# A graph network layer pair on one core: two neighbour runs per couple of units, a longer gather ring at the start, and a late stage cut into pieces

## What is computed

```python
hsrc = h[src]; coef = w_comp[etype]                    # 8 bases, 32 relations
msg = sum_b (hsrc @ weight[b]) * coef[:, b]            # times norm, one number per edge
node = relu(segment_sum(msg * norm, dst) + bias)
x = layernorm(x + node)
neigh = segment_sum(x[src] + edge_attr, dst)
h = ((1 + eps) * x + neigh) @ W1 + b1                  # 256 columns
h = relu(batchnorm(h) * gamma + beta)
out = layernorm(x + h @ W2 + b2)
```

## Time and profile before

| | |
|---|---|
| median of 3 runs | 603.48 us (603.25 to 607.04) |
| profiled execution, its time | 605.07 us |
| profiled execution, span | 603.3 us |
| PE busy | 507.7 us, 84% |
| DVE busy | 458.3 us, 76% |
| POOL busy | 401.1 us, 66% |
| ACT busy | 218.0 us, 36% |
| granted PE clock, mean | 0.885 |

### The profile page before, as it was taken

The page is one execution under the profiler, slowest core; times in us unless marked ns, Lnnn a source line. Parts: engine busy times, 40 slices in busy tenths (PEclk is TensorE's granted clock), DMA queues, the critical chain, the costliest instruction groups (busy, mean ns, idle before and its releaser), DMA issues.

```text
span 603.3 us, 12767 instructions
## 1 busy us (share of the span) xinstructions
PE 507.7 (84%) x3965; PEld 429.8 (71%) x3965; DVE 458.3 (76%) x1811; ACT 218.0 (36%) x323; POOL 401.1 (66%) x434
## 2 busy tenths in 40 slices
PE   4769888986868968878968899878899799899995
PEld 2459888776767657766757786767779699778775
DVE  6999999999885888877599887788844555527466
ACT  9904544453333242333333333422400000003276
POOL 5777777777777777777777777777777777720000
PEclk9986676997777996779997989978979899899999
DMA  5423756675664674665675868656667775843003
GB/s 131 123 55 93 246 187 181 208 258 167 195 199 139 205 229 141 200 216 197 193 242 185 269 166 292 178 196 212 227 195 234 221 225 153 265 127 109 3 2 107
DMA packets 98456, 108.18 MB, mean 179 GB/s; under 512 B 10949, under 2 KB 84918, under 8 KB 98386
## 3 DMA queue, kind: packets, MB, share of 16 engines
q1 hardware_dynamic: 79394, 77.81, 39.3%
q0 software_dynamic: 13312, 27.29, 16.0%
q10 hardware_dynamic: 5680, 2.23, 1.5%
HBM read 81.73 MB, written 25.56 MB: 178 GB/s over the span
## 4 chain that ended last, share of the span: by engine, by line
PE 47%; DVE 22%; DMA 17%; issue 5%; POOL 5%; SPq 1%; ACT 1%; DVEq 1%; POOLq 0%; ACTq 0%
PE psum L1218 16%; DMA gathered_flat<-in_x_dram,src_i 14%; PE psum L1135 10%; PE psum L1193 7%; DVE etype_hot L1610 5%; POOL gathered_flat L829 5%; PE psum L1128 5%; PE psum L1159 4%; DVE etype_hot L1607 3%; DVE sums_flat L1738 3%; DVE weighted L1495 2%; DVE adj_flat L1467 2%; DMA sums_flat<-in_x_dram 2%; PE psum L1361 2%; PE psum L1384 1%
## 5 line engine op out<-in xcount | busy, mean ns | idle before, releaser
L829 POOL DMA_INDIRECT gathered_flat<-in_x_dram,src_i x416 | 398.8, 959 | 129.8 <-issue 90.2
L914 ACT ACTIVATE adj_flat<-psum 128x500 f16<-128x500 f32 (+1 forms) x208 | 127.4, 612 | 236.0 <-PE psum L1159 226.7
L1135 PE MATMUL psum<-weighted,gathered_flat 128*128 128x96 f32 (+1 forms) x832 | 150.7, 310 | 39.5 <-DMA gathered_flat<-in_x_dram,src_i 39.4
L1135 PEld LDWEIGHTS psum<-weighted,gathered_flat 128*128 128x128 f32 x832 | 129.7, 218 | 45.0 <-DMA gathered_flat<-in_x_dram,src_i 44.9
L1128 PEld LDWEIGHTS psum<-hot,attrs 128*128 128x128 f32 x832 | 148.1, 217 | 12.3 <-issue 9.8
L1610 DVE TENSOR_SCALAR etype_hot<-iota_key,key_t 128x300 f16<-128x300 f16 (+1 forms) x416 | 136.0, 329 | 0.0
L1128 PE MATMUL psum<-hot,attrs 128*128 128x12 f32 (+1 forms) x832 | 133.2, 238 | 2.4 <-DVE weighted L1495 2.4
L1159 PE MATMUL psum<-etype_hot 128*128 128x300 f16 (+1 forms) x416 | 131.2, 344 | 2.5 <-DVE etype_hot L1610 2.5
L1607 DVE TENSOR_SCALAR etype_hot<-iota_key,gathered_flat 128x128 f16<-128x128 f16 x416 | 106.2, 255 | 22.3 <-PE psum L1159 15.5
L1738 DVE TENSOR_TENSOR sums_flat<-psum,sums_flat 128x180 f32 x208 | 71.1, 342 | 27.7 <-DVE sums_flat L1687 8.3
L1218 PE MATMUL psum<-sums_flat 128*128 128x264 f16 x630 | 83.7, 292 | 4.0 <-DVE weighted L1495 3.8
(11 more groups left out here) (158 smaller groups left out, 358.7 us busy)
## 6 DMA issues: line engine op xcount, KB each, us to landing
attrs<-in_edge_attr_dram SPq DMA_DIRECT2D x51, 512.0 KB
adjacency<-adj_flat SPq DMA_DIRECT2D x26, 900.0 KB
sums_flat<-adjacency SPq DMA_DIRECT2D x12, 576.0 KB, 5.5
gathered_flat<-in_x_dram,src_i POOLq DMA_INDIRECT x416
coef<-adjacency SPq DMA_DIRECT2D x21, 288.0 KB, 6.2
sums_flat<-adjacency SPq DMA_DIRECT2D x7, 432.0 KB, 5.5
sums_flat<-adjacency SPq DMA_DIRECT2D x10, 288.0 KB, 5.0
sums_flat<-adjacency SPq DMA_DIRECT2D x3, 504.0 KB, 8.5
```

Of the source, the lines that this page charges most:

```text
L829: pool.indirect_dma_start(gathered[:, t % (RING * GROUP), :], None, x[:, :], bass.IndirectOffsetOnAxis(src_i[:, t:t + 1], 0)).then_inc(gat ...
L914: nc.scalar.activation(window, counts, ACT.Copy).then_inc(counts_copied, 1)
L1135: nc.tensor.matmul(unit_psum(u)[:, 0:B, STARTS[i]:STARTS[i] + WIDTHS[i]], gathered[:, (u * UNIT + i) % (RING * GROUP), 0:F], weighted_tile ...
```

## The change

It has six parts.

1. **First columns direct** (`AHEAD = 2`): ACT loads the source indices of the first two tiles by two small DMAs straight into a column each (`src_slots`), and the first two gathers read those, instead of waiting for the chain that loads all indices as rows, turns them on PE and converts them on DVE (`src_i_ready`).
2. **Spare tiles** (`SPARE = 12`): tiles 32 to 43 are gathered into a piece of `sums` that isn't used yet; the ring goes on with tile 44. From tile 76 on the distance between a gather and the read that frees its place is 32 tiles, as before. ACT sets the piece back to zero after unit 21 (`zero_spare`), and two checks are added to the row of checks on DVE.
3. **Two runs per couple from unit 180** (`SECOND`): the planner goes by units instead of couples; from unit 180 PSUM banks 4 and 5 (free once all counts are done) take runs too, and a run may come one couple sooner behind its load. The plan has 62 runs with 276 tiles instead of 50 with 262. Up to the run of unit 179 it is the same.
4. **Early loads from step 46**: the four early `load_last` come one per step, at steps 46 to 49, instead of together at step 50.
5. **Late bases in two pieces**: the first 192 of the 309 late columns go through the bases at unit 202 (`LATE_STEP`), the other 117 behind the last unit. The last run has 2 tiles (6 before), the fills are 5 with 10 tiles (6 with 18), the finals 13 with 39 tiles (13 with 45).
6. **Late products wait chunk by chunk**: a final waits for the bf16 pieces of part 7 and of part 8 just ahead of the tiles that need them, and `turn_norm` of part 8 comes behind the first final. The adds of the runs of units 205 and 206 come behind the last unit's adds on DVE.

```diff
+SPARE = 12
+AHEAD = 2
...
+    LATE_STEP = U - 6
+    LATE_CUT = LATE_AT + 3 * P // 2
...
+    SECOND = 2 * ALL_COUNTED + 14
...
+    def run_bank_at(u):
+        if u % 4 == 2:
             return 7
+        if u % 4 == 3:
+            if u // 2 > ALL_COUNTED:
+                return 3
...
+        return 4 + u % 4 if u >= SECOND else None
...
-                if 2 * step + 2 + LEAD <= w:
-                    runs.append((w, b, reached[b], reached[b] + parts, place, step))
+                if 2 * step + 2 + LEAD - (u >= SECOND) <= w:
+                    runs.append((u, b, reached[b], reached[b] + parts, place, step))
...
-                    if g == GROUPS - 2:
-                        for b in LOAD_ORDER[0:EARLY_LOADS]:
-                            load_last(b)
+                    if 0 <= g - EARLY_STEP < EARLY_LOADS:
+                        load_last(LOAD_ORDER[g - EARLY_STEP])
...
+                if u >= FLYING + 4:
+                    pool.wait_ge(added, u - FLYING - 2)
+                if RU <= u < FLYING + RU:
+                    pool.wait_ge(gather_in[u % RU], u // RU * 16 * UNIT)
...
+                    if u >= FLYING + RU:
                         pool.wait_ge(tiles_read, t - RU * UNIT + 1)
+                    elif u >= FLYING:
+                        pool.wait_ge(tiles_read, t - FLYING * UNIT + 1)
...
+                        bass.IndirectOffsetOnAxis((src_slots if t < AHEAD else src_i)[:, t:t + 1], 0)).then_inc(gather_in[u % RU], 16)
...
+            for t in range(AHEAD):
+                act.dma_start(src_slots[:, t:t + 1],
+                              src[t * P:(t + 1) * P].rearrange("(p a) -> p a", a=1)).then_inc(weights_in, 16)
...
+            def zero_spare():
+
+                act.wait_ge(tiles_read, FLYING * UNIT)
+                nc.scalar.activation(sums[:, 0, SPARE_AT:SPARE_AT + SPARE * F],
+                                     zero_col[:, 0:1].to_broadcast([P, SPARE * F]), ACT.Copy).then_inc(zeroed, 1)
...
+                def late_bases(piece):
+
+                    first, last = ((LATE_AT, LATE_CUT), (LATE_CUT, N))[piece]
+                    for b in range(B):
+                        product = nc.tensor.matmul(psum[:, late_bank(piece), 0:last - first], w_base[:, b, :],
+                                                   sums[:, b, first:last], start=(b == 0), stop=(b == B - 1))
+                    product.then_inc(bases_mm, 1)
...
+                        if k in LATE:
+                            pe.wait_ge(parts_ready, k + 1)
...
+                    if u == LATE_STEP:
+                        pe.wait_ge(added, LATE_STEP)
+                        pe.wait_ge(x1_kept, LOOPED)
+                        late_bases(0)
...
                 pe.wait_ge(added, U)
-                bases(LOOPED, 0, B)
+                late_bases(1)
...
-                for k in LATE:
-                    turn_norm(k)
+                turn_norm(LOOPED)
                 for n in range(FILL_COUNT, len(FINALS)):
                     final_products(n)
+                    if n == FILL_COUNT:
+                        turn_norm(LOOPED + 1)
```

141 lines of the change are left out of this document (82 added, 59 removed).

## The result

| | before | changed |
|---|---|---|
| median on the same chip | 605.29 us (10 runs) | 601.28 us (10 runs, 598.43 to 604.72) |
| ratio, 95% interval | | 0.9942 [0.9922, 0.9962] |
| measured again, with the experiments | 604.33 us (35 runs) | 601.74 us (12 runs), 0.9957 [0.9933, 0.9980] |
| profiled execution, time and span | 605.07, 603.3 us | 599.79, 598.0 us |

The change is faster, by 2.6 to 3.5 us; the forecast was 9.3. By its own bound this is "within 1%", and the time lies above the range.

The account below looks back on a forecast made before the run. PE's own work was taken as the bound from unit 150 to 201, with the gather stream as floor up to the last unit. -5.8 us up to T and -3.9 behind it, 0.4 added back, gave -9.3: 594.2 us, range 591.5 to 599.5.

Parts of the forecast that it names:

- The start: First gathers: the third comes near 7 us and all later ones 2.4 us sooner (bounds 1.5 and 2.7).
- Unit 150 to 202: 8.2 us more run tiles, 5.2 us saved around unit 182's gap; PE starts unit 202 at 522.3 instead of 524.15.
- rival (2): Units 180 to 206: denser plan makes PE wait for DVE, 13 couples at 0.4 us; 599.4 us; 0.20 together with (4).
- (4): Ahead of the last unit: moved tiles only lengthen it, unit 182's gap stays; 598.4 us; 0.20 together with rival (2).
- Unit 202 to the last: Last units, with the first late piece added: they end at 534.4 instead of 537.33, -2.9 us.
- gather floor: Up to the last unit: the gather stream, 1.264 us each, lets it end at 534.4, one us above PE's own end.
- Behind the last unit: Wait for DVE's adds 1.0 instead of 1.30 us, bases 2.0 instead of 4.43, ACT's step 0.2 less.
- T: The end of `turn_back`, behind the last unit and late bases: forecast 538.4 instead of 544.2.
- From T on: T to the hidden layer: 6.1 us fewer tiles, 3.9 kept; finals end at T + 19.8 against 23.7 before.
- The sum: Whole kernel: -5.8 and -3.9, 0.4 added for small waits, -9.3 us; 594.2 by median, 595.8 for the profiled execution.
- (1): At the start: early gathers don't come, columns late or coefficient products hold the stream; 596.6 us; chance 0.12.
- (3): From unit 180 on: run loads come late and make it slower, 609.8 us; chance 0.06.

Follow-up runs that it names:

- e4: Changed kernel without parts 1 and 2 (old chain for the first columns, no spare tiles): 603.96 us, ratio 1.0005.
- e26: The fastest version (e22) without parts 1 and 2 (direct first columns, spare tiles): 597.71 us, ratio 0.9878.
- c1: The changed kernel measured and traced once more, nothing edited: 601.74 us, ratio 0.9957 to the kernel before.
- e1: Changed kernel with the last run's window adds on DVE between the late residuals and the late layer norm: 600.48 us, ratio 0.9955.
- e9: Changed kernel with part 6 undone on PE (both turn_norm and all late pieces ahead of the first final): 603.20 us, ratio 0.9970.
- e6: Changed kernel with the late bases in one piece of 309 columns behind the last unit: 607.03 us, ratio 1.0031.
- e17: Changed kernel with bases read once and the last run's adds between late residuals and late layer norm: 596.48 us, ratio 0.9851.
- e22: Changed kernel with bases read once, last run behind unit 207, its adds ahead of the residuals, first late piece behind unit 203: 593.58 us, ratio 0.9832.
- e16: Changed kernel with DVE reading the 26 window bases into registers once, at couple 88, instead of for each run: 597.00 us, ratio 0.9854.
- e3: Changed kernel without part 3 (old plan of 50 runs, six fills), all other parts kept: 600.24 us, ratio 0.9946.
- e2: Changed kernel with the last run right behind unit 207 and its adds ahead of the late residuals: 602.98 us, ratio 0.9983.
- e15: Changed kernel with the read of all 26 bases moved from behind the last unit to couple 100: 605.68 us, ratio 1.0018.

## Why the prediction was wrong, point by point

**The start** held in the main: third gather 7.07 (about 7), last 528.57 (528.5). The second was in part luck: in the sixteen traces with the whole start the last gather stands between 528.57 and 529.99, and this is the earliest, against 530.19 to 531.32 in the three without. It is worth 1.1 us alone (0.2 to 2.1), 2.9 us in the changed kernel (e4) and 2.8 us in the fastest version (e26): the last two fit the forecast's 2.4, the first lies below it. "All but 1 us would be given back" without the spare tiles was too mild: all was.

**Unit 150 to 202** is the step that failed. It said PE is "the bound by its own work", and priced each moved tile at PE's 0.34 us alone. From unit 180 to unit 202 that gives 49.7 us (472.06 to 521.73 before) + 8.2 - 5.2 = 52.7 us. The changed kernel takes 54.9 us in both traces. Up to unit 196 it needs 41.6 us, even 0.5 less than the same sum gives; from there to unit 202 it needs 13.3 instead of 10.6, and that is the wait of 1.7 us for DVE's matrices ahead of the run of unit 198 and the lower clock behind it. The second term is the shift: PE was to be at unit 180 at 472.06 - 2.4 = 469.7. In the first trace it is there at 467.51, which hides the missing 2.2 us and gives 522.41 for unit 202 (forecast 522.3): luck. In c1, e1 and e9 it is there at 471.0, 472.0 and 470.8, and unit 202 starts at 525.9, 526.9 and 525.2.

What was wrong is the use of DVE's busy time, 35.56 of 67 us, as room. In elapsed time a couple with two runs takes DVE 3.88 us, and the dense plan leaves PE no gap in which the lateness from before unit 180 goes. My rival (2) named the engine, and its 599.4 us is nearest to the result (0.9942 of 603.48 is 600.0). Its form was another, 13 waits of 0.4 us, where the trace has one of 1.7, two of 1.0 and 1.6 us around the late pieces, and the clock behind them. It got 0.20 together with (4), because of "PE may run two couples ahead"; but an engine that may run ahead waits as soon as the other is late for long.

**Unit 202 to the last.** The first piece took 2.87 us (2.9), the second 2.04 (2.0). That the two together take 0.5 us more than one, and not the 1.7 us more that the rule on LDWEIGHTS of the Trainium skill ("TensorE: Matmul & The Clock Gate") would give, is borne out where the clock is full: 4.91 against 4.43 us (6.54 in c1, with the second piece at the lower level). But the piece was not covered by the gather floor, since PE was not waiting for gathers; it covered DVE's backlog instead, as the 4.63 us of e6 show.

**Behind the last unit.** Forecast T 538.4; 539.5 in the first trace, 544.6 in the second, 544.3 in e9. The wait of "about 1.0" was 1.61, because the unit's adds stand behind four adds at 0.51 us and the read. In c1 and e9 part of the second piece goes at the lower clock behind it (3.67 and 2.74 us instead of 2.04). Moving the adds of units 205 and 206 behind the last unit's, which I costed at nothing, put the read of 26 bases onto the path: the late residual starts 0.8 us behind T (not in c1 and e9, where T is later).

**From T on.** The fifth fill came at T + 4.2 (4.7). The first final did not start at about 5.4 us but at 7.9, since its bank is the last run's; I had looked for the bank of the second final only. In the trace of the changed kernel that cost 3.3 us with the low clock behind it, in c1, where the gap is 2.02 us and the clock stays full, 0.8 us: tail 20.6. The executions differ here, and the experiments on the bank (e1, e17) found no gain that can be measured.

**The sum.** In c1, term by term against the forecast: unit 202 is 3.6 us late (1.3 of it already at unit 180, 2.3 from the stage behind that), the end of the last unit 3.9, T 6.2 (0.6 by the wait, 1.6 by the clock), and the tail adds 0.8. Less the 0.4 us that I had set aside, this is 6.6 us, and its execution has 602.42 us where the forecast has 595.8. In the first trace unit 202 is 0.1 us late, the end of the last unit 0.5, T 1.1, and the tail adds 3.3: with the 0.4 off 4.0 us, and its execution has 599.79 us. So the two executions lost their time in different stages. Over the three traces with the dense plan, all of the start and the old order of the adds (changed, c1, e9), T is 542.8 on average, 1.4 us below before, where I had 5.8; the tail is 21.8, 1.8 us below before, where I had 3.9. Together -3.2 us, near what was measured (-2.6 to -3.5), though one trace of before and a spread of 5 us in T don't bear more than that. A gain of the size of the forecast came only when the bases were read once and the last run and the first piece moved besides (e22: 0.9832, -10.1 us; the reads alone, e16: -8.8).

**The other rivals.** (1) did not come for the columns, which landed in time, though the shift reached unit 180 only in part. (3) did not come: no run from unit 180 on waited for its load; loads of 288 KB landed in 5.1 and 5.8 us. (4) held in its first half, as e3 shows: the moved tiles gained nothing, though not by a gap at unit 182, which was filled.

## What to carry to other kernels

Cost a step on the helper engine by the spacing of its instructions in the timeline, with the "issue" time ahead of them, and compare it per round with the round of the engine that it serves; a share of busy time under 60% can be an engine without room (DVE here: 38.20 of 67 us). A gap in the bound engine's row is also where it catches up: before filling it, see how late it enters the stage, and in more than one execution. And when a count changes (six fills to five), walk every cyclic resource by its index, here the PSUM banks, up to the first use whose holder is released behind other work.

## What the runs showed of the hardware that I had not expected

- Reading 26 window bases into DVE's registers takes about 2 us in which DVE does nothing (2.04 in e2, 2.07 in e15), and the reads for the two runs of a couple 1.0 us. None of it appears in the timeline as a row, or as busy time.
- With the bases kept in registers, four adds follow each other in 1.50 us (e16); with fresh ones they take 1.83 (three times 0.51, and 0.30). With fresh bases the trace has a register operation of DVE's sequencer ahead of every add shown (`FUSED_REGOPS`, 0.06 us), with kept ones it has none ahead of the four that take 1.50 us.
- Gaps of nearly the same length ahead of the first final left the clock full (2.02 us, then 27 products in 3.21 us) or at the lower level of 1.2 GHz (2.06 us in e6, then 27 products in 4.98 us; 2.67 us in the changed kernel, granted clock 0.50 from 549 to 551). So a tail with a gap of 2 us has two lengths, 20.6 us in c1 and 23.4 us in e6, and one trace tells only one of them. The same holds for the gap of 1.61 us ahead of the second late piece: 2.04 us for the 16 products at the granted clock 1.00 in the first trace, 3.67 us at 0.53 in c1.
